# Decoder layer on one core: other PSUM banks for the products of the chunk loop, and another order of instructions on four engines

## What is computed

```python
# 1: gated slot attention, 4 heads, 64 slots, a recurrence over the tokens
q, k, v = swish(x @ Wq), swish(x @ Wk), x @ Wv
f = log_sigmoid(x @ Wf) / 8;  s = 1 - exp(f)
hk = hk * exp(f) + k s^T;  p = softmax(q hk / 8);  hv = hv * exp(f) + s v^T;  o = p hv
o = o * rsqrt(mean(o * o) + eps) * g_norm;  out = o @ Wo
# 2: cross attention, 16 heads of 16, 64 context rows, a bias from positions, a mask
attn = exp(scores - max) / (1 + sum(exp(scores - max)));  out = (attn @ V) @ Wo
# 3: mixture of 8 experts, the best 2, capacity 1280 rows each
h = silu(xe @ W1) * (xe @ W3);  ye = h @ W2     # gathered, weighted, added
```

## Time and profile before

| | us |
|---|---|
| median of 3 runs (1373.56 to 1379.21) | 1374.69 |
| profiled execution | 1375.09 |
| its span | 1373.1 |

### The profile page before, as it was taken

One profiled execution on the slowest core, in us unless ns is written; L12 is line 12 of the kernel. 1 busy time (PEld: TensorE's weight loads), 2 busy tenths in 40 slices (PEclk: granted clock), 3 DMA queues, 4 the chain that ended last, 5 costly groups with the idle time before them and its releaser, 6 DMA issues.

```text
span 1373.1 us, 33453 instructions
## 1 busy us (share of the span) xinstructions
PE 1287.4 (94%) x11099; PEld 1139.0 (83%) x11099; DVE 930.4 (68%) x2770; ACT 640.0 (47%) x1628; POOL 420.2 (31%) x741
## 2 busy tenths in 40 slices
PE   7899999999999999998599999999999999999996
PEld 5677777777777777776379999999999999999996
DVE  5688888888888888887546565565645656565442
ACT  2555465555555555554335344443434535444331
POOL 4214443443444344333312222222221222222223
PEclk9999999999999999999689999999999999999999
DMA  8600301010101010100052252522524334352222
GB/s 246 181 19 26 126 27 35 26 34 27 34 26 35 27 35 26 34 23 21 28 138 32 32 123 32 124 32 35 128 37 118 37 67 92 36 124 32 32 25 24
DMA packets 152458, 80.18 MB, mean 58 GB/s; under 512 B 106210, under 2 KB 145859, under 8 KB 152290
## 3 DMA queue, kind: packets, MB, share of 16 engines
q1 hardware_dynamic: 137698, 59.11, 17.1%
q0 software_dynamic: 14592, 18.91, 8.2%
HBM read 44.04 MB, written 33.96 MB: 57 GB/s over the span
## 4 chain that ended last, share of the span: by engine, by line
PE 81%; DVE 7%; ACT 6%; issue 4%; POOL 0%; DMA 0%; POOLq 0%; ACTq 0%; DVEq 0%
PE banks L1391 33%; PE banks L1699 32%; PE banks L1500 4%; PE banks L1385 3%; PE banks L1575 2%; PE banks L1586 2%; PE banks L1495 2%; ACT qk_l L807 1%; ACT qk_e L805 1%; PE banks L1571 1%; DVE r_st L939 1%; DVE hk L1064 1%; ACT p_t L727 1%; DVE s_s L1047 1%; ACT one_less L817 1%
## 5 line engine op out<-in xcount | busy, mean ns | idle before, releaser
L912 ACT ACTIVATE h_a<-banks 128x256 f32<-128x256 f32 x320 | 122.3, 382 | 334.3 <-PE banks L1699 321.8
L1322 DVE TENSOR_TENSOR h_f<-banks,h_a 128x256 f32<-128x256 f32 x320 | 135.6, 424 | 138.0 <-ACT h_a L912 116.8
L528 POOL TENSOR_TENSOR idle_g<-half 128x1 f32<-128x1 f32 x144 | 31.5, 219 | 516.3 <-DVE y_s L1341 367.3
L1699 PE MATMUL banks<-xe_t_hi,w_even_hi 128*128 128x256 f32 (+1 forms) x640 | 178.6, 279 | 3.3 <-issue 1.8
L1699 PE MATMUL banks<-xe_t_lo,w_even_hi 128*128 128x256 f32 x640 | 178.2, 278 | 0.0
L1699 PE MATMUL banks<-xe_t_hi,w_even_lo 128*128 128x256 f32 x640 | 178.0, 278 | 0.0
L1699 PE MATMUL banks<-xe_t_hi,w_odd_hi 128*128 128x256 f32 (+1 forms) x640 | 177.7, 278 | 0.0
L1699 PE MATMUL banks<-xe_t_lo,w_odd_hi 128*128 128x256 f32 x640 | 177.4, 277 | 0.0
L1699 PE MATMUL banks<-xe_t_hi,w_odd_lo 128*128 128x256 f32 x640 | 177.3, 277 | 0.0
L901 ACT ACTIVATE h_t_hi<-h_f 128x256 fp32r<-128x256 f32 x320 | 131.7, 412 | 33.9 <-DVE h_f L1322 33.9
L707 POOL DMA_INDIRECT out_dram<-y_s,token x80 | 130.9, 1636 | 26.9 <-issue 20.0
(11 more groups left out here) (246 smaller groups left out, 3393.6 us busy)
## 6 DMA issues: line engine op xcount, KB each, us to landing
raw<-in_w SPq DMA_DIRECT2D x24, 1024.0 KB, 8.7
expert_rows<-empty SPq DMA_DIRECT2D x4, 2580.0 KB, 11.1
x_blocks<-expert_rows SPq DMA_DIRECT2D x312, 32.0 KB
xin<-in_x SPq DMA_DIRECT2D x32, 128.0 KB, 2.2
out_dram<-x SPq DMA_DIRECT2D x32, 128.0 KB, 1.7
out_dram<-y_s,token POOLq DMA_INDIRECT x80, 4.0
mask_i<-in_mask SPq DMA_DIRECT2D x32, 32.0 KB, 1.9
expert_rows<-r_xn,send POOLq DMA_INDIRECT x64, 2.7
```

The costliest lines, as they stand in the source:

```text
L528: return pool.tensor_tensor(idle_g[:, i:i + 1], half[:, 0:1], half[:, 0:1], ALU.add)
L912: act.activation(h_a[:, f % 2, :], bank[2 + f % 4][:, 0:GS], ACT.Silu).then_inc(silu_ok, 1)
L1322: dve.tensor_tensor(h_f[:, f % 2, :], bank[2 + f % 4][:, GS:2 * GS], h_a[:, f % 2, :], ALU.mult)\
L1699: last = pe.matmul(to[:, m * GS:m * GS + cols], lhs, rhs[:, at:at + cols], start=(i == 0), stop=(i == len(pairs) - 1))
```

## The change

`turns` is replaced by two tables: `written`, the order in which TensorE writes the products in one step, and `homes`, the bank of each. `bank_left` goes back in `written` from the product to the last one that has the same bank, and waits for that one's reader alone (further back only where that one isn't there in the first or last chunks). `scores1` waits in the first chunk for the context values that borrow its bank. Two adjacent banks each are kept for the pairs that VectorE reads as one (x_scores, scores, mix), `two_banks` becoming a function of the name.

The lists `step` of TensorE, VectorE, ScalarE and POOL are reordered, with some lags changed by one where a piece moves past the end of a list (`LAGS` 5 to 6): `r_columns` goes from behind `values` to the end of the list before, `send_rows` one list later. No piece is added or taken out, and each engine's instructions per chunk are the same but for the waits.

```diff
-LAGS = 5
+LAGS = 6
-        turns = [
-            [("read", 1), ("counts", 4), ("e_cols0", 2)],
-            [("mix0", 1), ("qk", 0), ("scores0", 0)],
-            [("mix1", 1), ("f_cols", 0), ("decay_cols", 0), ("scores1", 0)],
-            [("r_cols", 4), ("vf", 0), ("ks_cols", 0), ("logits", 0)],
-            [("values", 3), ("sums", 1), ("o_cols", 1)],
-            [("p_cols", 1), ("x_scores0", 2)],
-            [("xq", 2), ("x_scores1", 2), ("gates", 0), ("y", 1), ("e_cols1", 2)],
-            [("r_logits", 4), ("xy", 3), ("x_cols", 1)],
-        ]
+        written = [
+            ("values", 3), ("r_logits", 4), ("f_cols", 0), ("xq", 2), ("p_cols", 1), ("vf", 0),
+            ("mix0", 1), ("mix1", 1), ("counts", 4), ("x_scores0", 2), ("x_scores1", 2), ("read", 1),
+            ("qk", 0), ("xy", 3), ("gates", 0), ("sums", 1), ("o_cols", 1), ("decay_cols", 0),
+            ("ks_cols", 0), ("y", 1), ("scores0", 0), ("scores1", 0), ("e_cols0", 2), ("e_cols1", 2),
+            ("logits", 0), ("x_cols", 1), ("r_cols", 3),
+        ]
+        homes = dict(
+            values=0, r_logits=3, f_cols=5, xq=6, p_cols=7,
+            vf=1, mix0=4, mix1=5, counts=7, x_scores0=2,
+            x_scores1=3, read=7, qk=0, xy=5, gates=6,
+            sums=4, o_cols=3, decay_cols=2, ks_cols=1, y=3,
+            scores0=6, scores1=7, e_cols0=4, e_cols1=0, logits=1,
+            x_cols=4, r_cols=2,
+        )
+            i = [t for t, _ in written].index(name)
+            for k in range(1, len(written) + 1):
+                j = (i - k) % len(written)
+                other, other_lag = written[j]
+                if homes[other] != homes[name]:
+                    continue
+                m = n + lag_of[name] - other_lag - (1 if j >= i else 0)
+                if m >= 0:
+                    pe.wait_ge(left[other], min(m, NCH - 1) + 1)
+                if 0 <= m < NCH:
+                    break
+            if n == 0 and name in context_in:
+                pe.wait_ge(*context_in[name])
```

More of the change, by code:

```diff
@@ new lines, in decoder_layer @@
+        homes = dict(
[6 more added lines that the diff above has]
+        )
+        lag_of = dict(written)
+        tile = {t: bank[b][:, :] for t, b in homes.items()}
+        last_rows = [bank[7][:, 0:D], bank[1][:, 0:D]]
@@ L315, in over_chunks @@
                     behind(c)
+        context_in = dict(scores1=(v_made, B // 4))
         def bank_left(pe, name, n):
[L319 to L329, removed]
+            i = [t for t, _ in written].index(name)
[11 more added lines that the diff above has]
+                pe.wait_ge(*context_in[name])
         def over_groups(eng, step):
@@ L679, in step @@
             def step(run):
+                run(4, values)
+                run(6, send_rows)
+                run(2, keys)
+                run(1, both_gates)
+                run(2, head_power)
                 run(4, r_power)
-                run(3, values)
+                run(2, hidden_keys)
                 run(2, x_power)
                 run(0, f_power_later)
[L684 to L688, removed]
             over_chunks(step)
@@ L781, in context_keys @@
                     for k in range(KT):
-                        last = act.activation(k_all[:, k, :], tile[KEYS_AT[k]], ACT.Copy)
+                        last = act.activation(k_all[:, k, :], bank[keys_in[k]], ACT.Copy)
                     last.then_inc(k_made, 1)
@@ L873, in step @@
                 run(3, e_columns)
[L874 to L877, removed]
+                run(4, r_columns)
             def split_weights(e, par, piece):
@@ L1264, in step @@
             def step(run):
+                run(1, log_gates)
                 run(3, x_maximum)
@@ L1268, in step @@
                 run(2, head_outputs)
-                run(1, log_gates)
-                run(5, places)
-                run(2, end_states)
+                run(4, residual2)
+                run(4, r_statistics)
                 run(1, queries_keys)
                 run(1, slot_values)
-                run(4, residual2)
-                run(4, r_statistics)
+                run(2, end_states)
                 run(1, states_and_values)
@@ L1400, in context_keys @@
                 for m in range(KT):
-                    last = product(tile[KEYS_AT[m]],
+                    last = product(bank[keys_in[m]],
                                    [(xw[:, 1, k, m * P:(m + 1) * P], ctx_s[:, k, :]) for k in range(KT)])
@@ L1406, in context_values @@
             def context_values(part):
+                if part == 1:
+                    pe.wait_ge(left["decay_cols"], 1)
+                if part == 3:
+                    pe.wait_ge(v_made, B // 2)
                 for b in range(part * B // 4, (part + 1) * B // 4):
-                    last = product(tile[VALUES_AT[b // 2]][:, b % 2 * D:(b % 2 + 1) * D], [
+                    last = product(bank[values_in[b // 2]][:, b % 2 * D:(b % 2 + 1) * D], [
                         (ctx2[:, k, b, :, :].rearrange("p a k -> p (a k)"), xw[:, 2, k, :]) for k in range(KT)])
@@ L1466, in sum_states @@
                 pe.wait_ge(v_ok, n + 1)
[L1467 to L1468 removed]
+                pe.wait_ge(qk_ok, n + 1)
+                pe.wait_ge(s_ok, n + 1)
                 bank_left(pe, "sums", n)
@@ L1671, in step @@
                 run(1, x_columns)
+                run(3, r_columns)
             over_chunks(step)
```

61 lines of the change are left out of this document (32 added, 29 removed).

## The result

The changed kernel takes 1360.86 us (median of 4 runs, 1359.97 to 1362.27) against 1374.12 us before (4 runs, 1373.26 to 1379.21): a ratio of 0.9898, with a 95% interval of 0.9876 to 0.992. The profiled execution has a span of 1359.2 us against 1373.1. Of these 13.9 us head, loop and tail together make 12.2, and the expert phase, in which nothing was changed, 1.7 (671.9 us from its first product at 687.32 to the end, against 673.6).

A forecast was written before the change was run, and what follows sets the result against it. The old chunk loop was bound by TensorE and VectorE waiting for each other, the new by xy, VectorE's block and logits. Loop -20.1, head +0.7, tail -3 gave -22.4 us: forecast 1352.5 us, range 1332 to 1368.

The forecast's parts named there:

- three terms: Forecast changes: chunk loop -20.1 us (30 passes from 19.71 to 19.04), head +0.7, tail -3; total -22.4 us.
- The bound: Chunk loop: xy, the whole of VectorE's block and logits, back to xy, bound the pass at 19.14 us before fewer waits.
- The other loop: Loop through VectorE's block before xy, 8.23 us, within 0.1 of xy and so as tight.
- the new ring: Chunk loop: xy ends at 8.09, VectorE's block takes 5.95, masked logits start at 14.29, next vf at 19.14 us.
- 0.10 for fewer waits: Chunk loop: shorter bank waits between TensorE's groups taken as 0.10 us a pass, giving 19.04.
- +0.7, bounds -2 and +3: Head: f_norm before slot_logits (+0.4 on that chain) and later small tables, counted as +0.7 us in all.
- The tail: After the loop: counts, sums and xy no longer wait, about 3 us back; net -3, bounds 0 and -6.
- places: VectorE, chunk loop: place_h no longer meets POOL's g_both, so places is 0.52 us cheaper, 1.03 instead of 1.55.
- A: Chunk loop: TensorE goes to its own floor, pass 18.4, kernel 1334 us; chance 0.20.
- B: Chunk loop: place_h stays slow or VectorE's block gets a second wait; pass 19.45, kernel 1365 us; chance 0.15.
- C: Chunk loop: POOL blocks VectorE at three meetings of 0.45 us; pass 20.4, kernel 1393 us; chance 0.07.
- D: Gain goes in head or tail; both unfavourable bounds (+3, 0) give 1358 us; chance inside the forecast's 0.58.

The follow-up runs named there:

- `zk` alone: The changed kernel with the first product of the states waiting for zk only, no longer for zv: 1356.41 us, ratio 0.9852 to the kernel before.
- fewer waits alone: The kernel before, old order and banks, each product waiting only for the last writer of its bank's turn: 1378.54 us, ratio 1.0019.
- the keys late: The changed kernel with ScalarE's context_keys moved from in front of f_absolute to behind ks_columns: 1357.72 us, ratio 0.9866 to the kernel before.
- the shared bank: The changed kernel with the decays' columns put in the bank of the second half of the scores: 1361.95 us, ratio 0.9889 to the kernel before.
- the banks alone: The kernel before with the new banks and new rule of waiting, but the old order on all engines: 1374.81 us, ratio 0.9989.

## Why the prediction was right, and where it was off

The forecast was 1352.5 us in a range of 1332 to 1368, and the measured 1360.86 lies inside. The sum was -22.4 us, and -13.9 came. Its three terms were -20.1, +0.7 and -3; they measured -15.45, +5.5 and -2.25. Another -1.7 came from the expert phase, which was to stay as it was: that is luck.

*The bound.* Right. The pass is the loop of `xy`, VectorE's block and the logits. By its parts: `vf` to the end of `xy` 8.17 us (349.35 - 341.18), forecast 8.09; `xy` to VectorE 0.20, as forecast; masked logits to `vf` 4.75, forecast 4.85. VectorE's block with the step to TensorE took 355.67 - 349.55 = 6.12 us, forecast 6.00. Sum 19.24, measured 19.25. TensorE's order has no wait in brackets but the one named, at 0.31 us where 0.5 was given. The other loop was as near as forecast: `b_o`, the last instruction of the block before `xy`, starts 0.42 in front of `residual2`, where neighbours that don't wait start 0.34 apart, so it had 0.08 us to spare. That is why `places` put back shows at once.

*What the order replaced.* The prediction prices the new ring and takes the old pass as measured. The trace before shows what that one was made of:

```profile
346.95 1.94 PE L1391 MATMUL banks<-w_in,f_xnt 128*128 128x512 f32 x4
...
366.83 1.94 PE L1391 MATMUL banks<-w_in,f_xnt 128*128 128x512 f32 x4
```

```profile
350.36 0.42 DVE L1028 SCALAR_TENSOR_TENSOR g_s<-banks,f_l 128x256 f32<-128x256 f32 x1 [0.52 <-ACT f_l L800]
```

From `vf` over ScalarE to `log_gates` (`g_s`) 3.41 us; from there VectorE has no pause to `a_s` at 357.53, 7.17, with the long `place_h` among it; and from `a_s` over the logits to the next `vf` 9.30. The sum is 19.88, the pass. In the first chunk of a sequence `place_h` is short and the states are only cleared, the middle part is 6.23, and the pass 18.94. In the new order the path comes into VectorE's list only at `residual2`, behind `log_gates`, and `places` stands at the list's end. That is read from the traces; apart from `places` and `x_statistics` no piece of VectorE's list was moved alone.

*The size of the loop's gain.* 4.7 us short, in terms of a tenth of a microsecond that count thirty times. The mean pass was to be 19.04 and is 19.20. VectorE's block gives 0.12 of it, and nearly all of that is one dependent instruction: I priced `end_states` at the distance of its neighbours, 0.33 an instruction, but in the new order nothing stands between `zv` and the states that wait for it, and `hk` starts 0.45 behind `zv`. The run with `zk` alone moved the pass by that 0.10. `xy`, 0.08 later than the neighbouring starts gave, is the rest; one pass in four is 19.05, which takes some 0.05 off the mean. The "0.10 for fewer waits" may be the 0.10 by which masked logits to `vf` was shorter than forecast, but that isn't shown: with fewer waits alone the pass shrank by 0.04.

*The head.* This is the step that failed: "+0.7, bounds -2 and +3", measured +5.5. I looked at VectorE's list and not at ScalarE's, where the same edit put `context_keys` in front of `f_absolute`. In the first chunk its input comes at 16.16 us. The second `a_s` of three traces takes it apart: 43.08 with the keys late against 42.78 before, +0.3, which is left for everything else in the head, `f_norm` before `slot_logits` among it (0.7 was given); 45.73 with the keys early and the clock high, +2.65, the order on ScalarE; 48.29 with the clock at half, +2.56. Counted from the last product before the context's (11.70 us in the kernel before, the others as given above), the three are 0.8, 1.8 and 3.0: the parts are known to within a microsecond. Without the dip of the clock the head would have been +2.95, just inside the bound.

*The tail.* -2.25 against -3, and by the mechanism given: `counts`, the sums and `xy` run at once, and `o_cols` comes 15.67 us after the last `a_s` where it came 17.96 after it. The split before `x_xnt` takes 1.89 us of ScalarE (648.01 to 649.90), but TensorE waits only 0.21 us for `x_xnt` behind it.

*places.* Right. `place_h` is 0.165 in all chunks, and with the old place it is long again, exactly where `g_both` runs beside it, in 14 chunks of 32. The Trainium skill (SBUF — State Buffer, Who interferes with whom) says that such a pair blocks, the later one until the other is done; the runs agree, with 0.71 beside 0.72, ended 0.03 us apart. `off_f`, which has a single tensor input, was held as well; neither forecast nor expectation reckoned with that.

*The rivals.* A (TensorE's floor of 18.4) is refuted: the wait within the logits is there, fewer waits alone give nothing, and the pass less its wait is still 18.9 (19.25 - 0.31). B (pass 19.45) is what the passes with the long `place_h` are with `places` put back; their mean with the others is 19.39. C (POOL blocks VectorE) doesn't occur: `s_s` is 0.42 us long, `hid` starting 0.54 behind it, beside `zk`, which has one of its inputs in PSUM and is 0.42 too; `b_p`, `hot` and `both` keep 0.42, 0.17 and 0.17. D's two bounds were the right place to look, and its +3 was too near.

*Sums.* Three figures of the prediction don't follow from what it lists. VectorE's block before `xy` adds up to 8.13 and not 8.23, TensorE's floor to 18.1 and not 18.2, and the 0.84 for "faster" counts 0.06 of B's 0.15 where the text says "most of B". None of them changes the forecast.

*What stays open.* Why the expert phase took 1.7 us less: among the ten profiled executions its time differs by up to 6.4 us, without any edit to it. And how often the head's clock falls.

## What to carry to other kernels

A wait that goes away gives back only what lies between it and the next one: ask what else the waiting engine needs, and when that comes, before you price it. In a loop whose engines wait for each other in a ring, price the ring instruction by instruction, and give an instruction that waits for its neighbour its full latency. And read the list of each engine for the first pass on its own: a one-time step that is harmless in the steady state stands in front of everything when the pipeline is empty.

## What the runs showed of the hardware

After nearly the same waits in the head TensorE's clock fell in one execution and not in another. The changed kernel was busy 0.94 us from 18 to 20 us and 0.93 from 20 to 22, and then ran at 1.2 GHz until 28 us; with `zk` alone it was busy 0.80 and 0.93 there and stayed at 2.4 (granted 1.00). The dip cost some 2.6 to 3.0 us up to the second `a_s`. Three other kernels with the keys early (places back, the shared bank, `x_statistics` later) show it too: 0.66 from 20 to 30 us. So it came in four of five executions with the keys early, and in none of the five with the keys late (1.00 from 20 to 30 us in each): the order may bring it on, but one execution of each doesn't show that. The kernels with the banks alone and with fewer waits had a dip as well, at another place: 0.77 and 0.78 between 40 and 50 us, where the kernel before shows 1.00, and in both the second pass took 21.1 and 21.0 us against 18.9 there. So in one execution the head of this kernel is known to no better than 2 us, and a comparison of single profiles has to look at the clock first.

Small VectorE instructions on SBUF were held by POOL for as long as POOL's instruction ran: `place_h` 0.71 for 0.165 us beside `g_both`, and `off_f` and `send` 0.53 and 0.47 for 0.17 and 0.16 beside `k_bd`, in the kernel with `places` put back. A VectorE instruction of 0.42 us started 0.33 to 0.34 behind a neighbour that it didn't wait for, and the states 0.45 behind the neighbour that they did wait for.
